# Cross-attention over a 1601-key context on one Trainium2 core: chunks, slots and order of the work changed

## What is computed

```python
# per batch b of 8; 16 heads of 32; q from 64 positions, k and v from 1601 context rows
q = x @ Wq + bq;  k = ctx @ Wk + bk;  v = ctx @ Wv + bv
rel = clip(j - i, -32, 32) + 32                    # i: query, j: key
scores = (q . k + q . rel_k[rel]) * 32 ** -0.5
attn = softmax(scores)                             # over 1601 keys
out = attn @ v + attn @ rel_v[rel]
y = out @ Wo + bo
```

## Time and profile before

| what | us |
|---|---|
| median of 3 runs | 1698.22 (1698.11 to 1698.51) |
| the profiled execution's own time | 1694.82 |
| its span | 1692.8 |
| PE busy in the span | 1464.5 (87%) |
| ACT busy | 488.9 (29%) |
| DVE busy | 817.9 (48%) |
| POOL busy | 539.7 (32%) |

### The profile page before, as it was taken

One profiled execution on the slowest core, in us unless ns is written; L12 is line 12 of the kernel. 1 busy time (PEld: TensorE's weight loads), 2 busy tenths in 40 slices (PEclk: granted clock), 3 DMA queues, 4 the chain that ended last, 5 costly groups with the idle time before them and its releaser, 6 DMA issues. The chain is left out here.

```text
span 1692.8 us, 29730 instructions
## 1 busy us (share of the span) xinstructions
PE 1464.5 (87%) x12488; PEld 1094.1 (65%) x12488; DVE 817.9 (48%) x1649; ACT 488.9 (29%) x832; POOL 539.7 (32%) x340
## 2 busy tenths in 40 slices
PE   8788977477988999999999999999999966936796
PEld 3556755244544788888888888888888843415573
DVE  2455289989434343243333333323333215978913
ACT  0323201041112115252342523434243351303302
POOL 6101057657322232232322222232322104616701
PEclk9788965688999999999999999999999988967997
DMA  5300020010102412111021111102111024003000
GB/s 233 149 1 1 25 112 1 0 69 0 75 0 80 152 47 62 35 40 57 26 64 32 44 52 39 54 30 57 39 43 40 2 85 191 0 0 119 0 0 25
DMA packets 54514, 88.19 MB, mean 52 GB/s; under 512 B 28784, under 2 KB 45424, under 8 KB 51312
## 3 DMA queue, kind: packets, MB, share of 16 engines
q1 hardware_dynamic: 54384, 86.31, 14.9%
HBM read 76.60 MB, written 9.70 MB: 51 GB/s over the span
## 5 line engine op out<-in xcount | busy, mean ns | idle before, releaser
L1058 POOL TENSOR_TENSOR ctx_hi<-ctx_raw,one 128x1024 fp32r<-128x1024 f32 (+1 forms) x48 | 94.5, 1970 | 590.6 <-issue 546.9
L1315 DVE TENSOR_TENSOR V<-PS,vbias 128x512 f32<-128x512 f32 (+1 forms) x104 | 71.8, 691 | 366.0 <-PE PS L1098 365.8
L1243 ACT COPY ET<-PS 128x512 f32<-128x512 f32 (+1 forms) x224 | 130.4, 587 | 287.5 <-PE PS L1158 287.4
L1349 DVE TENSOR_SCALAR_CACHE_REDUCE E<-PS 128x256 f32<-128x256 f32 (+1 forms) x384 | 141.1, 433 | 90.7 <-PE PS L1134 90.2
L1088 PE MATMUL PS<-ctx_hi,wk_hi 128*128 128x256 f32 (+1 forms) x768 | 139.9, 304 | 6.7 <-issue 6.7
L1158 PE MATMUL PS<-ident,E 128*128 128x128 f32 (+1 forms) x832 | 132.1, 284 | 13.2 <-ACT E L1250 12.5
L1088 PE MATMUL PS<-ctx_lo,wk_hi 128*128 128x256 f32 (+1 forms) x768 | 126.8, 287 | 0.0
L1088 PE MATMUL PS<-ctx_hi,wk_lo 128*128 128x256 f32 (+1 forms) x768 | 125.4, 285 | 0.0
L1225 ACT ACTIVATE K<-PS,kbias 128x256 f32<-128x256 f32 x160 | 76.1, 475 | 170.4 <-PE PS L1088 170.4
L1250 ACT ACTIVATE E<-E,peak 128x1601 f32<-128x1601 f32 x64 | 103.4, 1621 | 66.2 <-DVE peak L1354 66.2
L1061 POOL TENSOR_TENSOR ctx_lo<-ctx_raw,ctx_hi 128x1024 fp32r<-128x1024 f32 (+1 forms) x48 | 119.8, 2496 | 3.8
(11 more groups left out here) (282 smaller groups left out, 2415.2 us busy)
## 6 DMA issues: line engine op xcount, KB each, us to landing
ctx_raw<-in_ctx SPq DMA_DIRECT2D x40, 512.0 KB, 3.7
ctx_raw<-in_ctx_first SPq DMA_DIRECT2D x8, 644.0 KB, 3.9
rel_scr<-rel_out SPq DMA_DIRECT2D x8, 640.0 KB, 4.0
fwk<-in_fwk SPq DMA_DIRECT2D x1, 4096.0 KB, 12.4
fwv<-in_fwv SPq DMA_DIRECT2D x1, 4096.0 KB, 12.8
corr<-rel_scr SPq DMA_DIRECT2D x64, 48.0 KB
p_scr<-E SPq DMA_DIRECT2D x16, 192.0 KB, 2.1
near<-p_scr SPq DMA_DIRECT2D x64, 48.0 KB
```

Of the source, the lines that this page charges most:

```text
L1058: nc.gpsimd.tensor_tensor(ctx_hi[r][:, :, 0:n], ctx_raw[r][:, :, 0:n], one[:].unsqueeze(1).broadcast_to([P, KC, n]), ALU.mult).then_inc(S[ ...
L1243: nc.scalar.copy(ET[0:n, j % ET_RING, :], src[0:n, :]).then_inc(S["et_out"], 1)
L1315: v.tensor_tensor(V[0:rows, at % V_RING, :], bank(4 + (b * NU + i) % 2)[0:rows, :], vbias[0:rows, :], ALU.add).then_inc(S["v_out"], 1)
L1349: v.tensor_scalar(E[:, p, k0:k0 + n], bank(r)[:, at:at + n], 1.0, None, ALU.mult, ALU.max, accum_out=tops[:, p, c:c + 1]).then_inc(S["s_ou ...
```

## The change

The context is cut in four chunks (449 keys, then three of 384), so a batch has 16 K and 13 V units, and `K` is four tensors of which two share memory. `ctx_lo` is written over `ctx_raw`, so a load now waits until the chunk two before it has been projected. A unit is issued in two halves of six products; the list of a period is laid out in slots, one for each half. Score jobs are one half of the heads of a chunk each, eight jobs of 16 products. `corr` is single. The inverse is made without diagonal matrices: one transpose of the [128, 8] inverses, a copy by ACT, two products with a selection matrix, a second copy by ACT; both steps stand at the end of the period's list. In the last batch the K units of all chunks are in period 7 and the V units of all chunks in period 8, for which the chunks are loaded and split a second time; period 7 has two turns in a slot, all on bank 6, and period 8 two turns in a slot on banks 6, 0 and 1.

```diff
-CH = 256
+CH = 384
-FIRST_CH = FIRST + 2 * P
+FIRST_CH = FIRST + CH
+S_JOBS = [(c, o) for c in range(NCH) for o in range(OCT)]
+VISITS = [(b, c, "kv") for b in range(B - 1) for c in range(NCH)] + [(B - 1, c, kind) for kind in "kv" for c in range(NCH)]
...
+def period(p):
+
+    slots = 2 * len(UNITS[p])
+    at = [[] for _ in range(slots + 8)]
+    put = lambda slot, item: at[min(slot, slots + 7)].append(item)
+    if p == B - 1:
+        turns, lag, scored = (lambda j: 16 + j // 2), 1, (21, 22, 24, 25, 27, 28, slots, slots)
+    elif p == B:
+        turns, lag, scored = (lambda j: 12 + j // 2), 1, ()
+    else:
+        turns, lag, scored = (lambda j: 13 + 44 * j // T_GROUPS), 2, (26, 28, 36, 38, 46, 48, 54, 56)
+    if p >= 1:
         for kt in range(P_GROUPS):
+            put(max(turns(2 * kt + 1) + lag, 2 * kt + 4 if p == B else 0), ("p", kt))
+        for j in range(T_GROUPS):
+            put(turns(j), ("t", j))
+    for job, slot in enumerate(scored):
+        put(slot, ("s", job))
     out = []
+    for slot in range(slots + 8):
+        out += sorted(at[slot], key=lambda item: "pts".index(item[0]))
+        if slot < slots:
+            out.append(("u", slot))
+    if p >= 1:
+        out += [("r", 0), ("r", 1), ("norm", 0)]
+    return out
...
-    ctx_lo = [m.tensor(f"ctx_lo{r}", [P, KC, (FIRST_EVEN, CH)[r]], F32R) for r in range(2)]
+    ctx_lo = [m.rounded(f"ctx_raw{r}") for r in range(2)]
...
         if q >= 2:
-            sp.wait_ge(S["split_lo"], q - 1)
+            wait_projected(sp, q - 2)
...
+            for p, ba, items in PERIODS:
                 for c in range(NCH):
+                    q = p * NCH + c
+                    if 2 <= q:
                         load_ctx(sp, q)
+                    if ba >= 0 and c == {B - 1: 3, B: 2}.get(p, 1):
                         exchange_near(sp, ba)
+                    if c == 3 and p + 1 < B:
+                        load_corr(sp, p + 1)
+            for q in range(len(VISITS) - 2, len(VISITS)):
+                wait_projected(sp, q)
...
             def turn(b, j):
                 last_batch = b == B - 1
-                dst = bank((BANK_T, 4, 5)[j % 3] if last_batch else BANK_T)
+                dst = bank((BANK_T, 0, 1)[j % 3] if last_batch else BANK_T)
...
+            def spread_inverse(b, step):
+                if step == 0:
+                    pe.wait_ge(S["et_out"], T_GROUPS * (b + 1))
+                    pe.wait_ge(S["inverted"], b + 1)
+                    last = nc.tensor.transpose(bank(BANK_T)[0:PAIRS, 0:P], inverse[:], s.ident[:])
+                else:
+                    pe.wait_ge(S["r_out"], 2 * b + 1)
+                    pe.wait_ge(S["l_small"], 16 * 7)
+                    for o in range(OCT):
+                        last = nc.tensor.matmul(bank(BANK_T)[:, o * P:(o + 1) * P], sel[:, o, :], inverse_rows[:], start=True, stop=True)
                 last.then_inc(S["r_ps"], 1)
...
+            def inverse_copy(b, step):
+                act.wait_ge(S["r_ps"], 2 * b + step + 1)
+                if step == 0:
+                    nc.scalar.copy(inverse_rows[:], bank(BANK_T)[0:PAIRS, 0:P]).then_inc(S["r_out"], 1)
+                else:
+                    if b >= 1:
+                        act.wait_ge(S["normed"], b)
+                    nc.scalar.copy(spread[:], bank(BANK_T)[:, 0:OCT * P]).then_inc(S["r_out"], 1)
...
                     elif kind == "t":
                         turned(ba, k)
                     elif kind == "s" and k == len(S_JOBS) - 1:
-                        exponentials(bp)
+                        exponentials(p)
                     elif kind == "r":
-                        inverse_copy(ba)
+                        inverse_copy(ba, k)
```

More of the change, by code:

```diff
@@ L855 @@
[L855 to L861, removed]
-        for kt in range(P_GROUPS):
-            out += [("p", kt)] + [("t", j) for j in (2 * kt + 3, 2 * kt + 4) if j < T_GROUPS]
-        return out + [("r", 0), ("norm", 0)]
-    out = []
[L866 to L880, removed]
+    return range(0, TPC + 1) if c == 0 else range(TPC * c + 1, TPC * (c + 1) + 1)
@@ new lines, in units_of_visit, with on_dve @@
+def units_of_visit(q):
+    b, c, kinds = VISITS[q]
+    ks = [("k", q, b, c, g) for g in range(KC)] if "k" in kinds else []
+    vs = [("v", q, b, c, kt) for kt in tiles_of_chunk(c)] if "v" in kinds else []
+    return vs + ks if q == 0 else ks + vs
+VISITS_OF = [range(p * NCH, (p + 1) * NCH) for p in range(B + 1)]
+UNITS = [[u for q in VISITS_OF[p] for u in units_of_visit(q)] for p in range(B + 1)]
+ORDER = [u for units in UNITS for u in units]
+NUMBER = {u: n for n, u in enumerate(ORDER)}
+def on_dve(unit):
+    kind, q, b, c, j = unit
+    return kind == "k" and (c == 0 or (b == B - 1 and c == 1))
@@ L883, in cross_attention @@
+PERIODS = [(p, p - 1, period(p)) for p in range(B + 1)]
 def cross_attention(nc, sem, s, nm):
@@ L904, in cross_attention @@
     ET = m.tensor("ET", [P, ET_RING, D])
[L905 removed]
+    corr = m.tensor("corr", [P, PAIRS, EDGE])
     near = m.tensor("near", [P, PAIRS, EDGE])
@@ L1094, in unit @@
                     k0 -= keys_of_chunk(c)[0]
-                    pe.wait_ge(S["v_lo"], 1)
-                    for w, x in ((wv_hi, ctx_hi[r]), (wv_lo, ctx_hi[r]), (wv_hi, ctx_lo[r])):
-                        for kc in range(KC):
-                            last = nc.tensor.matmul(dst[0:rows, :], x[:, kc, k0:k0 + rows], w[:, kc, :],
-                                                    start=(k == 0), stop=(k == 3 * KC - 1))
-                            k += 1
-                    last.then_inc(S["v_ps"], 1)
+                    products = [(dst[0:rows, :], x[:, kc, k0:k0 + rows], w[:, kc, :])
+                                for w, x in ((wv_hi, ctx_hi[r]), (wv_lo, ctx_hi[r]), (wv_hi, ctx_lo[r])) for kc in range(KC)]
+                half = len(products) // 2
+                for k in range(half * second, half * (second + 1)):
+                    last = nc.tensor.matmul(*products[k], start=(k == 0), stop=(k == 2 * half - 1))
+                if second:
+                    last.then_inc(S[kind + "_ps"], 1)
             def relative(b):
```

309 lines of the change are left out of this document (133 added, 176 removed).

## The result

The changed kernel takes 1795.99 us (median of 4 runs, 1790.4 to 1796.37) against 1698.37 us for the kernel before (4 runs, 1698.11 to 1699.04). The ratio is 1.0566 (95% interval 1.0546 to 1.0587): **97.6 us slower**. The forecast was 1787 us, with a range of 1762 to 1820.

A forecast was written before the change was run, and what follows sets the result against it. The prediction took PE's instruction stream as the bound. Period 0 -2, periods 1 to 6 +78, periods 7 and 8 +11 and next-layer weights +1.7 gave +88.7 us on 1698.2: 1787 us, range 1762 to 1820.

The forecast's parts named there:

- the deciding step: End of periods 1 to 7: PE waits at r1 for ACT's copy behind the exponentials, idle 11.8 us in periods 1 to 6.
- the first rival: At r1: no wait, because ACT copies r0 while waiting for the maxima; 1685 us, faster; chance 0.05.
- The sum of a period: Each of periods 1 to 6: -1.1 + 11.8 + 2.3 = +13.0 us, six of them +78.
- the small terms: Periods 1 to 6: K products -0.5, breaks and halves +0.9, PE's own waits -1.5; together -1.1 us a period.
- The half clock: Behind each idle at r1, PE work runs at half clock: 2.0 us lost plus 0.3 for r1's products.
- Period 0: First period: about 3 us wait for the third chunk, earlier 4.0 us wait gone, K products -0.5; taken -2 us.
- The chain of 10.9 us: Load and both splits of a chunk, run as one chain behind the projection two before; cost taken 0.6 us.
- Periods 7 and 8: From period 7's start to the normalised end: idle 30.3 us against 18.8, products and breaks -0.8; taken +11 us.
- the term for `w3o`: After the last V unit: PE waits for the next layer's weights, whose loads come late; +1.7 us (0 to 4).
- No wait at r1: At r1: ACT copies r0 while waiting for the maxima, so PE doesn't wait; 1685 us; rival, chance 0.05.
- A ladder of waiting turns in periods 1 to 6: Turns with only a half unit between them wait in ordinary periods too: +36 us, 1823 us; rival, chance 0.13.
- A shorter wait: At r1: the wait exists but is shorter by, say, 4 us each; 1760 us; rival, chance 0.06.

The follow-up runs named there:

- e1: Changed kernel with both steps of r directly ahead of the last score job in periods 1 to 7: 1687.34 us, ratio 0.9938 to the kernel before.
- e3: Kernel before the change with the item r moved behind the last score job, all else as before: 1772.32 us, ratio 1.0438.
- e5: Changed kernel with unread PE products issued during the wait at r1, 16 in each of periods 1 to 6 and 19 in period 7: 1785.84 us.
- e2: Changed kernel with unread PE products issued during the wait at r1, 32 in each of periods 1 to 6 and 36 in period 7: 1837.55 us.
- e8: e1 plus, in period 7, a weigh between two turns and turns spread over slots 11 to 29; in period 0 third chunk loaded before corr: 1680.47 us.

## Why the prediction was right, and where it was off

**The bound and the deciding step.** PE was the bound, the softmax's chain was hidden, and r behind the last score job brought it to light. Predicted idle 11.8 us, measured 11.91; for period 7 predicted 15.4, measured 15.57. The wait ends where the prediction said, with a copy of 0.24 us (taken 0.3) right behind the eighth exponential. e1 takes the position alone away and the loss is gone, e3 puts the position alone in and it is there: the cause is shown, not only argued.

**ACT keeps its order.** This was read from one row of before, the copy at 1375.41, and the Trainium skill's "strict FIFO" ("Perfetto Trace Analysis", section "Tensor Engine Instruction (MATMUL, LD_WEIGHTS)") agrees. ACT was free for 6.78 us ahead of the exponentials of period 7, while r0 was done 2.4 us before they began, and didn't take the copy: the first rival's condition was met and it didn't happen.

**The sum of a period.** Predicted +13.0 us, so 117.2; measured 117.75. Without the wait -1.1 was predicted; e1 has 103.2 against 104.2, and 0.34 of that is the short wait that is left, so -1.3. That holds the small terms together: K groups of 384 columns at 0.70 us (predicted 0.70) and of 450 at 0.82, more breaks, and PE's own waits down from 1.55 us to 0.35. The columns cost what the rows said; no run has larger chunks alone, so what they are worth by themselves isn't measured. The half clock was the term that was mis-sized: 2.3 us taken (bounds 1.6 and 3), 2.8 to 3.0 by e5, e2 and e1, which is half of the 6.0 us for which it lasted on average. I took it near the row of 3.2 us at half clock behind 4 us of idle; behind 11.9 us of idle it lasted 4.8 to 7.3 us, as long as the longer row or longer. Of the 0.7 us a period that this adds, the small terms make good 0.2.

**Period 0.** Predicted -2, measured -1.2. The wait for the third chunk was 1.48 us in place of 3. The wait for corr was read wrongly: the 4.0 us of before are that wait (DVE's first score addition is let go by the corr load there), it was counted as gone, and it only shrank, to 2.71. The chain of 10.9 us is also more than its three terms, which add up to 10.6; the medians of the changed kernel are 4.3, 2.75 and 3.49, together 10.5.

**Periods 7 and 8.** With the wait for `w3o` predicted +12.7, measured +16.7. Windows of this stretch, after and before:

```profile
1335.80:1501.41 165.61, 134.29 (x1607) 104.21 (x1607) 33.73 (x94) 50.64 (x85) 38.31 (x12) 0.92 0.15 47
...
1257.71:1406.60 148.89, 129.77 (x1790) 107.59 (x1788) 40.77 (x143) 67.74 (x110) 21.46 (x11) 0.95 0.19 67
```

PE's idle time goes from 19.1 to 31.3 us, +12.2, where 11.5 and 1.7 for `w3o` were predicted. The waits are as predicted (14 of 0.68 against 0.67; 1.13 for the chunk against 0.6; 0.87 and 2.15 round s6 and s7 against 0.6 and 2.1), but the term for `w3o` came to nothing: PE waits 1.21 us for the load where 1.22 us stood before. What was mis-sized is PE's busy time: +4.5 us where -0.8 was taken. Of this, 2.0 are the half clock behind the sixth wait, which the prediction had booked with its six periods. The other 2.5 lie in the products and in the breaks between operations, which I took as no more than before. A slot with a weigh, two turns and a half K unit takes 3.55 us of which the wait is 0.68; no run takes its parts further apart.

**The layers behind.** Predicted nothing beside `w3o`. Measured +1.0 in all, of which more than all is the clock: the output layer's 32 products took 16.74 us where they took 13.97 before, and for the first 5.5 us the clock was 0.50, which accounts for the 2.8 between. PE had been idle for just 1.21 us right ahead of them.

**The rivals.** No wait at r1: refuted by the trace, and its price was right, 1685 us against 1687 measured in e1, where its condition is made true. A ladder of waiting turns in periods 1 to 6: not there; in the five periods of the window PE idles for 59.5 us, which is five times 11.91 and nothing beside. A shorter wait: no.

**What made it come out within the range, and 9 us low.** On the median the result is 97.6 us, the sum was 88.7. Seven of the nine are the terms above: period 0 +0.8; periods 1 to 6, with all of the half clock behind their six waits, +3; periods 7 and 8 without that half clock +2; the layers ahead and behind +1.3. The other two are that the timed runs lie 5.6 us above the profiled one, where for the kernel before it was 3.55 us. No large errors cancelled: the one that went the other way is the 1.7 us for `w3o`.

## What to carry to other kernels

Where several engines walk one list, a two-step exchange (PE, ACT, PE) must stand ahead of whatever long work the middle engine takes up in that stretch: look at what the other engines do between the two steps, not at what the steps cost. A softmax is hidden only as long as nobody needs its engine, or anything queued behind its engine, until it is done. When two turns share one buffer, put an operation that doesn't need it between them.

## What the hardware showed that was not expected

After the long idle stretches the clock was always at half for a while, as expected. But it was at half after short ones too, in the traces of some kernels and not of others. In period 0, where the programs of both are the same, after 2.71 us of idle the 16 score products took 1.01 us in the changed kernel and 1.80 in e1:

```profile
586.34 1.01 PE L1145 MATMUL PS<-K,qT 32*64 32x449 f32 x16 [2.71 <-DVE E L1357]
```

```profile
587.08 1.80 PE L1151 MATMUL PS<-K,qT 32*64 32x449 f32 x16 [2.71 <-DVE E L1363]
...
1334.72 1.58 PE L1151 MATMUL PS<-K,qT 32*64 32x384 f32 x16 [0.89 <-DVE E L1363]
```

The last row had only 0.89 us of idle before it, with 0.87 and 0.34 us a little earlier; in e8 the same 16 products, behind the same three waits, took 0.91 us at full clock. So waits that look harmless one by one can cost up to 3 us more, as ahead of the output layer, and differences of 2 or 3 us between kernels of this kind aren't to be read from one trace.
